# One-hot rows of a routed feed-forward written unit by unit, with unread matrix products placed anew

## What is computed

```python
x = x + tanh(g_xattn) * attention(layernorm(x), ctx, ctx, W, b)      # 77 context rows a sequence, masked
logits = layernorm(x) @ router_w.T                                   # 8 experts
top_w, top_i = top_k(softmax(logits), 2); top_w /= sum(top_w)
h = silu(xf @ w_gate[e].T) * (xf @ w_up[e].T)                        # xf = layernorm(x)
x = x + tanh(g_ffn) * sum over the 2 chosen e of top_w * (h @ w_down[e].T)
```

## Time and profile before

| | us |
|---|---|
| median of 3 runs (lowest, highest) | 419.22 (418.49, 422.79) |
| the profiled execution's own time | 420.82 |
| its span, first to last instruction | 419.1 |
| busy PE, DVE, ACT, POOL | 406.4, 311.4, 287.4, 280.6 |
| mean granted TensorE clock | 0.985 |

### The profile page before, as it was taken

The page is one execution under the profiler, slowest core; times in us unless marked ns, Lnnn a source line. Parts: engine busy times, 40 slices in busy tenths (PEclk is TensorE's granted clock), DMA queues, the critical chain, the costliest instruction groups (busy, mean ns, idle before and its releaser), DMA issues.

```text
span 419.1 us, 9883 instructions
## 1 busy us (share of the span) xinstructions
PE 406.4 (97%) x3211; PEld 377.1 (90%) x3211; DVE 311.4 (74%) x690; ACT 287.4 (69%) x585; POOL 280.6 (67%) x271
## 2 busy tenths in 40 slices
PE   8999899989999999999999999999999999999993
PEld 3788676556999999999999999999999999999993
DVE  6579978985877677777777777867777777777772
ACT  2489876364767776767777676777676777777672
POOL 7007574647377667777776766776777777777775
PEclk9999969999999999999999999999999999999998
DMA  6948875654876777543433333343334343333333
GB/s 184 346 153 276 283 241 181 228 178 119 289 166 144 176 180 167 127 62 52 63 64 64 51 55 60 56 68 66 52 51 63 51 63 64 64 51 56 59 60 63
DMA packets 34625, 50.26 MB, mean 120 GB/s; under 512 B 3846, under 2 KB 26023, under 8 KB 34599
## 3 DMA queue, kind: packets, MB, share of 16 engines
q0 software_dynamic: 13440, 19.19, 27.4%
q1 hardware_dynamic: 19815, 29.84, 22.5%
q10 hardware_dynamic: 1344, 0.92, 0.7%
HBM read 32.24 MB, written 17.70 MB: 119 GB/s over the span
## 4 chain that ended last, share of the span: by engine, by line
PE 45%; POOL 24%; issue 16%; DVE 6%; DMA 3%; ACT 2%; POOLq 2%; SPq 0%; ACTq 0%; DVEq 0%
POOL out_rows L523 15%; PE GT L1269 11%; PE UP L1269 11%; PE Y L1297 10%; POOL xt L511 8%; PE W L1114 3%; PE S L1139 3%; PE O L1188 2%; PE XT L1259 2%; DMA xg<-in_x 2%; DVE xg L911 1%; DMA out_rows<-y,idx 1%; POOLq L60 1%; POOLq L540 1%; ACT ex L614 1%
## 5 line engine op out<-in xcount | busy, mean ns | idle before, releaser
L523 POOL DMA_INDIRECT out_rows<-y,idx x68 | 159.7, 2349 | 64.6 <-ACT y L685 51.1
L1057 DVE TENSOR_TENSOR gu<-raw,gu 128x1024 fp32r<-128x1024 f32 x70 | 85.8, 1226 | 62.7 <-ACT gu L661 58.4
L1269 PE MATMUL GT<-xtT,gu 128*128 128x256 f32 x828 | 113.4, 286 | 0.0
L1269 PE MATMUL UP<-xtT,gu 128*128 128x256 f32 x828 | 110.6, 283 | 0.0
L1269 PEld LDWEIGHTS UP<-xtT,gu 128*128 128x128 f32 x828 | 104.3, 192 | 0.0
L1269 PEld LDWEIGHTS GT<-xtT,gu 128*128 128x128 f32 x828 | 103.8, 191 | 0.1
L1297 PE MATMUL Y<-dn,hT 128*128 128x256 f32 x816 | 103.5, 283 | 0.0
L1297 PEld LDWEIGHTS Y<-dn,hT 128*128 128x128 f32 x816 | 100.4, 192 | 0.0
L511 POOL DMA_INDIRECT xt<-xn_rows,idx x74 | 75.2, 1017 | 27.4 <-issue 22.2
L661 ACT CAST gu<-raw 128x1024 fp32r x68 | 70.8, 1042 | 30.7 <-PE UP L1269 29.4
L1078 DVE TENSOR_TENSOR hid<-hid,UP 128x512 f32<-128x512 f32 x68 | 46.5, 684 | 9.7 <-PE UP L1269 9.7
(11 more groups left out here) (172 smaller groups left out, 396.8 us busy)
## 6 DMA issues: line engine op xcount, KB each, us to landing
raw<-in_weights SPq DMA_DIRECT2D x32, 384.0 KB
xn_rows<-pay SPq DMA_DIRECT2D x8, 528.0 KB, 3.4
xTg<-in_xT SPq DMA_DIRECT2D x8, 512.0 KB, 4.4
xg<-in_x SPq DMA_DIRECT2D x8, 512.0 KB, 6.2
out_rows<-xg SPq DMA_DIRECT2D x8, 512.0 KB, 4.1
xt<-xn_rows,idx POOLq DMA_INDIRECT x74
out_rows<-y,idx POOLq DMA_INDIRECT x68
kr<-in_ctx_rows SPq DMA_DIRECT2D x1, 308.0 KB
```

The lines of the kernel that those rows point to most:

```text
L523: gp.indirect_dma_start(out=out, out_offset=bass.IndirectOffsetOnAxis(ap=idx[:, 2 * j + t:2 * j + t + 1], axis=0), in_=y[:, j % 2, t, :], ...
L1057: return tt(out=out, in0=whole, in1=high.bitcast(F32), op=ALU.subtract)
L1269: last = mm(bank[:, h * PT:(h + 1) * PT], gu[:, pw, q, c, w, h * P:(h + 1) * P], xtT[:, b, px, c], start=(h == 0 and c == 0 and n == 0), s ...
```

## The change

at_low is laid out unit by unit. For each unit one VectorE tensor_scalar compares iota_p (now one copy of the numbers 0 to 127) with `low` and multiplies by the code, both given as one float32 number for each partition. The separate multiplication `coded` and its places in the loop and behind it are gone; low_ready is raised by the last of a group's eight instructions. `low` and `code` become float32. ScalarE's two lines and the list product address the new layout. The unread products ahead of the transposes number 0, 2, 3, 5, 4, 5, 6 for k = 0 to 6 where they were 0 and then 3 each; those ahead of the counts 18 where they were 22. The numbers of lines behind line 850 shift.

```diff
-        iota_p = sb("iota_p", [P, P, 2], F16, a)
+        iota_p = sb("iota_p", [P, P], F16, a)
-        code = sb("code", [P, GROUPS, TOPK, G], F16, a)
+        code = sb("code", [P, GROUPS, TOPK, G], F32, a)
...
-        low = sb("low", [P, UNITS], F16, a)
+        low = sb("low", [P, UNITS], F32, a)
...
-        at_low = sb("at_low", [P, UNITS // 2, P, 2], F16, a)
+        at_low = sb("at_low", [P, UNITS, P], F16, a)
...
-                nc.scalar.activation(apart[:, u], iota_p[:, :, 0], ACT.Square, bias=low_last[:, u:u + 1], scale=-1.0
+                nc.scalar.activation(apart[:, u], iota_p[:], ACT.Square, bias=low_last[:, u:u + 1], scale=-1.0
...
-                last = nc.scalar.activation(at_low[:, (UNITS - CU + u) // 2, :, u % 2], apart[:, u], ACT.Relu,
+                last = nc.scalar.activation(at_low[:, UNITS - CU + u], apart[:, u], ACT.Relu,
...
             def at_lows(k, lo, hi):
...
-                at = k * CU // 2
-                rows_hot[0] = mark(tt(out=at_low[:, at + lo // 2:at + hi // 2],
-                                      in0=iota_p[:].unsqueeze(1).to_broadcast([P, (hi - lo) // 2, P, 2]),
-                                      in1=by_two(low[:], k, lo, hi), op=ALU.is_equal))
-
-            def coded(k):
-
-                if k < 0:
-                    return
-                after(rows_hot[0])
-                of = at_low[:, k * CU // 2:(k + 1) * CU // 2]
-                tt(out=of, in0=of, in1=by_two(code[:].rearrange("p g c t -> p (g c t)"), k, 0, CU),
-                   op=ALU.mult).then_inc(low_ready, 1)
+                codes = code[:].rearrange("p g c t -> p (g c t)")
+                for u in range(k * CU + lo, k * CU + hi):
+                    last = ts(at_low[:, u], iota_p[:], low[:, u:u + 1], codes[:, u:u + 1], ALU.is_equal, ALU.mult)
+                if hi == CU:
+                    last.then_inc(low_ready, 1)
...
-                coded(behind)
...
-            coded(last_group - 1)
...
+            BUSY = (0, 2, 3, 5, 4, 5, 6)
...
-                if k > 0:
-                    keep_busy(3, ET)
+                keep_busy(BUSY[k], ET)
...
-            keep_busy(22, W)
+            keep_busy(18, W)
...
-                last = mm(L[:, LIST:LIST + TILES], at_low[:, u // 2, :, u % 2], at_tile[:, u // 2, :, u % 2], start=(u == 0), stop=(u == UNITS - 1))
+                last = mm(L[:, LIST:LIST + TILES], at_low[:, u], at_tile[:, u // 2, :, u % 2], start=(u == 0), stop=(u == UNITS - 1))
```

More of the change, by code:

```diff
@@ L452, in _ @@
             gp.iota(iota_e[:], [[1, NE]], base=0, channel_multiplier=0, **exact)
-            gp.iota(iota_p[:], [[1, P], [0, 2]], base=0, channel_multiplier=0, **exact)
+            gp.iota(iota_p[:], [[1, P]], base=0, channel_multiplier=0, **exact)
             gp.iota(iota_t[:], [[1, TILES], [0, 2]], base=0, channel_multiplier=0, **exact)
@@ L845, in low_places @@
                 v.tensor_copy(low[:, k * CU:(k + 1) * CU], low_i[:]).then_inc(places_ready, 1)
[L847 to L852, removed]
             def at_lows(k, lo, hi):
```

## The result

The changed kernel takes 423.31 us (median of 20 executions, 421.97 to 432.39) where the kernel before takes 418.90 (20 executions, 417.40 to 423.21). The ratio is 1.0107, with a 95% interval of 1.0088 to 1.0127: slower by 4.5 us. The forecast was 419.0 with a range of 416.0 to 422.5. The profiled execution of the changed kernel took 425.39 us, with a span of 423.6.

The account below looks back on a forecast made before the run. It took TensorE to bound the expert stage and VectorE's turns, with a slow clock stretch, to set its start. Profiled 420.82 us, less 3.0 for the clock, plus 1.2 for later turns, gave 419.0, range 416.0 to 422.5.

Parts of the forecast that it names:

- I take 0.16, the nearer row's: VectorE's new one-hot rows: each instruction takes 0.16 us, eight make 1.28 us a group.
- The upper 0.22 (each of the two pays 0.06): Upper end for one new one-hot instruction on VectorE, both per-partition operands charged: 0.22 us, 1.76 a group.
- The net per turn: VectorE's turn of a group: ve comes 0.42 us later, and what follows it 0.24 us later.
- The saving of the product: Between ve and rt0v on VectorE: taking the product out saves 0.18 us, since the wait for ScalarE stands behind it.
- Groups 3 to 7 do: 5 x 0.24 = 1.2 us: VectorE's delay is passed on by five groups at full clock, 1.2 us in all.
- Group 2 doesn't pass this on: Group 2's turn hides VectorE's delay, because ScalarE waits there 0.63 us for the load of x.
- The wait for GpSimd: One-hot instructions ahead of ve can wait for GpSimd: 0.15 us a group, bounds none and 0.6.
- The clock term: Added unread products keep TensorE's clock from falling near 55 us: worth 3.1 us, less 0.1 left over.
- slow stretch later: Rival: half clock returns at the tables' gap at 89.88 us and runs into the experts, 423.9 us; chance 0.07.
- The four less give nothing: Ahead of the counts, four fewer unread products save nothing, as VectorE's last one-hot rows end at 85.50 us in both.
- the last call: Last one-hot rows, ahead of own_ranks: 1.44 us before, 1.43 after, so nothing.
- The rival of costly instructions: Rival: eight one-hot instructions cost 1.76 us a group, with waits of 0.6; 424.5 us with the fall gone; chance 0.05.

Follow-up runs that it names:

- e3: Changed kernel plus 32 unread one-hot instructions between tables and list; 128 columns took 0.22, 0.16 and 0.10 us with two, one and no per-partition operands.
- e1: Kernel before with only the changed numbers of unread products; 418.99 us, ratio 1.0014.
- e9: Kernel before, two comparisons moved to the end of the turn ahead, and 0, 3, 3, 5, 5, 5, 6 unread products in the turns; 417.01 us, ratio 0.9952.
- e10: Repeat of e6: kernel before with two of four comparisons moved to the end of the turn ahead; 416.87 us, ratio 0.9968.
- e7: Changed kernel with the last one-hot pair moved behind low and the first pair to the end of the turn ahead; 418.32 us, ratio 0.9996.
- e5: Changed kernel with the last one-hot pair of each turn moved from ahead of ve to behind low; 420.35 us, ratio 1.0068.
- e8: Kernel before with four unread instructions without per-partition operands added ahead of ve in six turns; 421.50 us, ratio 1.0067.
- e6: Kernel before with two of its four comparisons moved to the end of the turn ahead, ahead of the reciprocal; 417.01 us, ratio 0.9976.
- e2: Changed kernel with the old numbers of unread products, so the one-hot rows alone; 422.95 us, ratio 1.0101.
- e4: Changed kernel with one per-partition operand instead of two in the turns, all units rewritten behind them; 432.65 us, group 6's turn 6.81 us.

## Why the prediction was wrong

From 419.0 to 423.3 are 4.3 us. They lie in these steps.

**"I take 0.16, the nearer row's" failed.** The instruction takes 0.22 us, the upper end. The masks of the earlier trace rows have one per-partition operand, and from them I had worked out 0.05 to 0.09 us for one. The new form has two, and I charged one: 0.16 is what e3 measured with one operand. "The upper 0.22 (each of the two pays 0.06)" was the sum that follows from my own rows, and e3 measured just these 0.06. Choosing the value of the nearest row was the mistake: a row that differs from the case by a known piece has to be corrected by it. So 1.78 us a group instead of 1.28. (The lower end of "0.16 to 0.19" should have been 0.15 by its own terms, which changes nothing.) With 1.76 in its place, and everything else as I had it, my own sum gives 0.72 us a turn and 3.6 for five turns, where 3.7 were measured.

**The net per turn was too small by the same piece.** I had ve 0.42 us later and what follows 0.24; in group 3 it was 0.77 and 0.66. The saving of the product, "0.18 us and not 0.60", had the right mechanism: rt0v waits for ScalarE. It came to 0.11 in group 3, 0.18 in group 4, 0.01 in group 6 and 0.29 in group 7.

**"Groups 3 to 7 do: 5 x 0.24 = 1.2 us" had the right groups.** It came to 3.7 by the turns, 2.5 of the 4.3. "Group 2 doesn't pass this on" held for the most part: its ve came 0.88 us later after its lg (3.71 to 4.59) and its turn was only 0.22 longer, no longer than e1's with the old rows.

**The wait for GpSimd, 0.15 a group, was of the right size and partly wrong in form.** It was 0.24 us a group in both kernels. In group 3 of the changed kernel the first pair ran within GpSimd's payload work and took 0.44 us, as undisturbed; in group 4 it took 0.67, 0.22 more, and ended ahead of GpSimd's instruction. What decides was not isolated.

**The clock term was booked against the wrong time.** "That the fall near 55 us doesn't come, worth 3.1 us" is right for the profiled execution. But of 64 executions of before in the three batches, 52 have a mean granted clock of 0.99 or more and a median of 418.3 us, and only 12 have less and a median of 420.9. A mean below 0.99 goes with 2.6 us more, near my 3.0, and with a fifth of the executions. So the median had next to nothing to give back. For the forecast's time this matters little: 420.82 - 3.0 = 417.8, where the undisturbed executions take 418.3, so 0.5 us of the error. But it hid from me that the forecast of "no change" was a saving that the median can't have against a loss that it has.

**And the fall doesn't stay away.** I said it would not come, because products would fill a gap down to 1.0 us. VectorE's delay, larger than I took, widened the gap to 1.46 in spite of them; the clock stayed full behind it in this profile, so the sign came true and not for my reason. In 6 of 19 executions of after, the mean clock is below 0.99, with a median of 424.2 us against 422.8 in the other 13. That lifts the median by some 0.5 us. The limit of 0.99 is coarse: the profiled execution has 0.990 and counts among the 13, though its clock fell at 90 to 94 us. There the rival "slow stretch later" had put it, and I had held against it that the gap of 1.48 us there doesn't change; it was 2.12. The stretch ended before the experts, so the list took 0.94 us longer and the experts started some 0.5 later, and not 4.9. That rival's case did occur once: in e3's only execution half clock from 105 to 111 us lay in the experts, which took 322.81 us instead of some 320.5.

**"The four less give nothing" was half right.** In time they gave nothing. But the counts of picks now wait 0.61 us for GpSimd on TensorE (at 85.25), a gap that the products had covered.

**Right:** the products cost nothing that could be measured in the median (e1; e9 against e10); the expert stage is untouched but for the wait of 3.66 us in this one profile. **Luck:** that the last call costs the list nothing. I had it at 1.43 us and it takes 1.99. What followed it on VectorE up to the first at_tile took 2.96 us instead of 3.51, which I hadn't seen coming.

These add up to 2.5 + 0.5 + 0.5 = 3.5 of 4.3 us. Group 2's 0.2 and the later start of the experts, 0.5, may be the rest, as said above, but neither is shown for the median. The rival of costly instructions named the cause, and I gave it 0.05: the masks spoke for it as much as for my value. Its 424.5 us went too far since it charged waits of 0.6 us in each group.

## What to carry to other kernels

Count the per-partition operands of a short VectorE instruction: at 128 columns they cost more (0.12 us for two) than the columns and all the rest (0.10), so a fused form in small pieces can lose against two wide passes. Before a clock event of one profile is booked as a gain, ask whether the unprofiled executions have it: their mean granted clock gives a hint. And ask where an instruction stands before asking what it costs: four moved instructions in each turn (e7) were worth as much as the whole loss.

## What the hardware showed beside it

- **The same program loses the clock in some executions only.** Mean clock below 0.99: before 12 of 64, products alone 1 of 13, rows alone 5 of 6, after 6 of 19, one pair moved (e5) 3 of 7, more work in before (e8) 6 of 10, e6 and e10 together 2 of 22, e9 0 of 12, e7 0 of 12. Kernels whose turns are longer tend to lose it more often, though e5's turns are shorter than after's. The added products seem to make it rarer (e2 against after, before against e1), but these counts are small.
- **The length of a single gap doesn't decide.** Before fell to half behind a gap of 1.22 us; after kept 1.00 behind 1.46 at 53.37 us, and fell behind 2.12. At the same place ahead of the list e5 kept full clock behind 2.12 us and e2 behind 2.01. Among the profiles the list ran at half clock in three of the five with 18 products ahead of the counts (after, e1, e7; not e3 and e5) and in none of the six with 22; e4 is left out, since its clock was low before. Whether the four products decide it was not tested.
- **The wait of 3.66 us** in the experts of after's profile came in none of the other profiles, and its cause is open.
